# Paired causal attentions on one core: three of a group's four key blocks summed in one visit to the 32-column part of the array

## The reference

```python
x = _layernorm(x + _L0_attn_ref(x, ...))      # causal, 16 heads of 8 channels, T = 256
...
# _L2_attn_ref
scores = jnp.einsum('bthd,bshd->bhts', q, k) / jnp.sqrt(HD)
scores = scores + alibi[None]
scores = jnp.where(causal[None, None], -jnp.inf, scores)
attn = jax.nn.softmax(scores, axis=-1)
out = jnp.einsum('bhts,bshd->bthd', attn, v).reshape(Bb, Ss, Dd)
return out @ Wo + bo
```

## Time and profile before

| | |
|---|---|
| median of 3 runs | 2263.75 us (2261.84 to 2269.63) |
| profiled execution | 2265.27 us, its span 2263.3 us |
| TensorE busy | 1973.9 us, 87% |
| VectorE busy | 1460.6 us, 65% |
| ScalarE busy | 1171.9 us, 52% |
| GpSimd busy | 813.2 us, 36% |

### The profile page before, as it was taken

How to read it: one execution, slowest core, us unless ns; L and a number is a source line. 1 busy time by engine, 2 the same in 40 slices (tenths; PEclk the granted TensorE clock), 3 DMA queues, 4 the chain that set the end, 5 groups by cost and what they waited for, 6 DMA issues and landing times.

```text
span 2263.3 us, 44486 instructions
## 1 busy us (share of the span) xinstructions
PE 1973.9 (87%) x17496; PEld 1179.8 (52%) x17496; DVE 1460.6 (65%) x2920; ACT 1171.9 (52%) x1950; POOL 813.2 (36%) x1153
## 2 busy tenths in 40 slices
PE   5886689998878989998999788999899898999888
PEld 2342466666644544554665344444555665666446
DVE  5775687878768777773555776121677676767464
ACT  2575356656622444555333467322576675757432
POOL 4544343433126748343001331000545344453033
PEclk7998799999989999999999899999999999999999
DMA  4430111111234434210201220000465564655152
GB/s 130 140 103 2 25 31 28 30 33 26 63 107 127 125 98 137 59 49 1 104 1 50 88 91 20 32 0 1 154 206 175 173 208 131 207 174 168 51 114 56
DMA packets 183990, 199.10 MB, mean 88 GB/s; under 512 B 55922, under 2 KB 152486, under 8 KB 179302
## 3 DMA queue, kind: packets, MB, share of 16 engines
q1 hardware_dynamic: 183782, 196.27, 29.5%
HBM read 93.53 MB, written 92.08 MB: 82 GB/s over the span
## 4 chain that ended last, share of the span: by engine, by line
PE 34%; DVE 6%; ACT 6%; issue 3%; DMA 2%; POOL 2%; SPq 1%; DVEq 0%; ACTq 0%; POOLq 0%
PE PS L2104 5%; PE PS L357 4%; PE PS L2351 3%; PE PS L2367 3%; PE PS L1957 3%; PE PS L2339 3%; ACT AR L2509 2%; PE PS L1944 2%; PE PS L1947 2%; PE PS L2703 1%; PE PS L604 1%; PE PS L2691 1%; PE PS L2693 1%; DMA AR<-ZD 1%; PE PS L583 1%
## 5 line engine op out<-in xcount | busy, mean ns | idle before, releaser
L1282 ACT ACTIVATE AR<-PS 128x1024 f32<-128x1024 f32 x160 | 162.6, 1024 | 123.9 <-PE PS L1031 123.0
L725 ACT ACTIVATE AR<-PS 128x1024 f32<-128x1024 f32 x160 | 162.9, 1024 | 93.3 <-PE PS L583 48.0
L1135 DVE TENSOR_REDUCE AR<-PS 128x2 f32<-128x768 f32 (+1 forms) x192 | 159.9, 864 | 55.8 <-PE PS L1011 30.7
L2565 POOL TENSOR_TENSOR RA<-AR,RA 128x288 f32<-128x288 f32 x128 | 88.2, 698 | 275.4 <-DVE RA L2441 142.2
L2509 ACT ACTIVATE AR<-PS,AR 128x512 f32<-128x512 f32 x256 | 174.0, 687 | 24.2 <-DVE AR L2430 24.0
L2430 DVE TENSOR_REDUCE AR<-PS 128x2 f32<-128x1024 f32 x128 | 156.8, 1225 | 12.9
L2339 PE MATMUL PS<-AR 64*128 64x200 f32 (+2 forms) x1280 | 147.0, 354 | 2.9 <-ACT AR L2509 2.9
L1828 POOL TENSOR_TENSOR AR<-AR 128x1024 f32<-128x1024 f32 x32 | 75.4, 2358 | 174.4 <-DVE AR L1676 174.4
L2351 PEld LDWEIGHTS PS<-CC,AR 64*128 64x128 f32 x2048 | 77.8, 140 | 98.1 <-issue 76.7
L2351 PE MATMUL PS<-CC,AR 64*128 64x64 f32 x2048 | 92.3, 229 | 38.7 <-DVE AR L2436 11.7
L2339 PEld LDWEIGHTS PS<-AR 64*128 64x128 f32 x1280 | 111.3, 193 | 6.3 <-ACT AR L2509 3.2
(11 more groups left out here) (366 smaller groups left out, 4984.4 us busy)
## 6 DMA issues: line engine op xcount, KB each, us to landing
ZD<-RC SPq DMA_DIRECT2D x32, 1152.0 KB
AR<-ZD SPq DMA_DIRECT2D x32, 640.0 KB
ZP<-AR SPq DMA_DIRECT2D x128, 160.0 KB, 2.7
SP<-AR SPq DMA_DIRECT2D x40, 384.0 KB, 2.6
AR<-SP SPq DMA_DIRECT2D x128, 96.0 KB
RA<-SP SPq DMA_DIRECT2D x32, 384.0 KB
SP<-AR SPq DMA_DIRECT2D x40, 256.0 KB, 2.9
RC<-RC SPq DMA_DIRECT2D x64, 130.0 KB
```

The source lines that it names most:

```text
L725: e.activation(self.PT[m % 6], C.PS[:, 2 * s:2 * s + 2, :], ACT.Exp).then_inc(S["s_turned"].sem, 1)
L1135: i = e.tensor_reduce(nm[:, :, 4 * up + q:4 * up + q + 1], src[:, :, a:a + wd], AX, ALU.max, negate=True)
L1282: e.activation(self.PT[m % 6], C.PS[:, 2 * s:2 * s + 2, :], ACT.Exp).then_inc(S["s_turned"].sem, 1)
```

## The change

`order` puts the key blocks 1, 3 and 2 of the group before into the list together, in the step with m % 5 = 1, where they stood one each in the steps with m % 5 = 0, 1 and 2. `take` stays in the step with m % 5 = 2. The items of `post` (pieces, proj, fin, turnx) come in the steps with m % 5 = 1 and 4, where they came in those with 1 and 3. Key block 0 stays in the step with m % 5 = 4. No instruction is added or taken away, and the order of the sums is the same.

```diff
@@ -501,9 +501,9 @@
             k = m // 5
-            if m >= 5 and m % 5 < 3:
-                plan.append(("group", k - 1, (1, 3, 2)[m % 5]))
-                if m % 5 == 2:
+            if m >= 5 and m % 5 == 1:
+                plan.extend(("group", k - 1, kb) for kb in (1, 3, 2))
+            if m >= 5 and m % 5 == 2:
                     plan.append(("take", k - 1))
                     if k % 4 == 0:
                         post += [[("piece", k // 4 - 1, q)] for q in range(NT)] + [[(s, k // 4 - 1)] for s in ("proj", "fin", "turnx")]
@@ -515,7 +515,7 @@
-            elif post and (m % 5 in (1, 3) or m >= N):
+            elif post and (m % 5 in (1, 4) or m >= N):
                 plan += post.pop(0)
```

## The result

The changed kernel takes 2293.1 us (median of 4 runs, 2290.4 to 2297.7) against 2266.7 us; the ratio is 1.0125, 95% interval 1.0102 to 1.0147. It is slower by 26 us, the way that was forecast, but 12 us above the forecast of 2280.7 and 2 us above the top of its range. Measured once more in a later series it took 2292.0 us, ratio 1.0122 (1.0102 to 1.0142). The profiled execution took 2290.4 us, its span 2287.4, 24.1 more than before.

A forecast was written before the change was run, and what follows sets the result against it. TensorE was taken to bound the kernel only while each step carries filling work. Uncovered waits less saved shape changes gave +9.9 us (second stage) and +7 (first), +16.9 on 2263.75: 2280.7 us, range 2264 to 2291 for 8 in 10.

The forecast's parts named there:

- Rival 1: Whole kernel: TensorE bounds and array-shape changes count; uncovered waits stay small, 8 us gained, 2256 us; chance 0.12.
- Rival 2: Both stages: new waits only replace existing waits for maxima and normalisation stalls; about 2268 us; chance 0.14.
- Rival 3: Merged visit itself waits for exp or select, 1 us in each first-stage group; 2296 us; chance 0.08.
- The price of a group: Second-stage group: 1.4 us of uncovered waits less 0.26 saved; +1.1 us where no wait was before.
- S3: Start of the `scores` matmuls in step m % 5 = 3; second stage: 0.45 us wait for the exp.
- S4: Start of the `scores` matmuls in step m % 5 = 4; second stage: 0.59 us wait, exp behind `take`.
- k 7: Second-stage group with proj in step 3: 1.1 us, plus 0.7 as `value` behind proj needs its bank cleared.
- k 1: First second-stage group counted: ends on DMAs of the start, so 0 us.
- k 2: Second-stage group where step 3 already had a 0.32 us wait: +0.8 us.
- k 12: Second-stage group where ScalarE's normalisation stall was to take in part of the new waits: +0.3 us.
- the sum: Adding group costs over both stages: +9.9 us in the second, +7 in the first, +16.9 in total.
- the terms that I took at nothing: Second stage's first group, steps without scores at its end, and turnx and proj moved in the last group: 0 us.

## Why the prediction was right in kind and short in size

**The bound and the rivals.** That TensorE is the bound only as long as each step is filled was right. Rival 1 (the shape changes decide) is refuted by the merged visit alone (1.0085); the shape change itself was sized right, at 0.14 us a visit in the kernel with two blocks joined and 0.28 us a group in the merged one, for 0.26 forecast. The Trainium skill (TensorEngine Tiling, Key Properties) says that a change of the tiling mode drains TensorE. The rows agree in that each change taken out saves 0.14 us; that it is a drain, they do not show. What it is worth depends on who is waiting. Rival 2 (absorbed) did not come: the maxima's waits fell from 9.7 to 4.8 us in the first stage, as foretold in kind, but they were not enough, and in the second stage they rose from 3.8 to 4.4. Rival 3 did not come: no row of the merged visit waits for the select.

**The price of a group.** Forecast 1.4 us of waits (0.35, 0.45, 0.59) less 0.26, measured 1.45 (0.33, 0.65, 0.47) less 0.28: +1.17 for +1.1. S3 was dearer than said, because step 2 takes 0.73 us when bare, not 0.83, and `scores` came 0.15 us behind the exp, not 0.06; S4 was cheaper by 0.12 us. Group by group in the second stage, from the `turned` of step 0, with the forecast in brackets: k 5 and 6 +1.17 each (1.1), k 7 +1.86 (1.8), k 8 +0.22 (0.3), k 9 +1.44 (1.1), k 10 +1.17 (1.1), k 11 +0.62 (0.8), k 13 +0.42 (0.8), k 3 and 4 together +0.59 (0.7). Far off are k 1, +1.36 (0), k 2, +1.80 (0.8), and k 12, +1.37 (0.3). In the first stage the four groups with a piece grew by 4.6 us (4.8).

**Where it failed.** The step that failed is the sum: the terms that I took at nothing or at 0.3 for the places where the norm, the transfers and the stage's end set the pace, and a term that it does not have at all, stretches at a low granted clock. By part, the second stage is +4.1, +8.1 and +1.9 us for 1.5, 7.6 and 0.8, and the first stage +9.6 for 7; in the second profile +4.7, +8.9, +2.2 and +8.3.
- k 12, second stage: +1.37 us for 0.3, at a granted clock of 1.00. I took ScalarE's stall for the norm to swallow part of the new waits. It is the other way round: the length of step 0 is set by the stall, and the 384 visit that stood in it had been free. It saves 0.15 us where it left and is paid in full in step 1. The move of `fin` by one step changes what `rows` waits for (`value`'s addition is queued behind the norm on VectorE, and `rows` behind the bank), but costs little: the moved pieces alone make +0.31 us in this group, the merged visit alone +0.80.
- k 12, first stage: +3.11 us. Step 0 is again 0.15 us shorter, but behind its wait of 2.37 us the merged visit runs at the lower of the clock's two levels. Timeline of TensorE and busy time by stretch (the clock is the third number from the end):

```profile
173.62 2.79 PE L604 MATMUL PS<-AR 128*32 128x384 f32 x24
173.62:176.33 2.71, 2.71 (x26) 0.98 (x24) 1.29 (x2) 0.55 (x1) 1.36 (x4) 0.50 0.05 11
```

It takes 2.71 us to the next instruction, for 1.43 at full clock. In the second profile the same came in k 12 of the second stage, 12.74 us for 11.11, with the visit at 2.69. In the first stage the group's mean granted clock is 0.73 to 0.88 in all six profiles of the kernels with the merged visit and the work in full, and 1.00 in all five of those without it.
- The first stage: its middle part grew by 10.9 us in one profile and 6.4 in the other. Besides k 12, the group k 4 grew by 2.09 us, with the 512 visit at a granted clock of 0.51 (1.86 us to the next instruction, for 1.00).
- The start of the second stage: +4.1 us, for 1.5 forecast. k 2 took 10.16 us at a granted clock of 0.83; the kernel with the norm put back, whose order is the same up to there, has 8.99 at 1.00. So 1.2 us of it go with the clock. The rest is k 1, which waits for the transfers, and part of both may be chance, as the moved pieces' kernel shows.
- The end of the second stage: +1.9 us for 0.8 (that of k 13). The 512 visit of the last group waits 3.37 us for `take`, which ScalarE does only after the square root of the third block's norm; that norm comes one step later, behind a proj that is one step later. The moved pieces alone show the same wait, 3.23 us. I had set this against the cover that the visit gives turnx. The last merged visit behind it runs at a granted clock of 0.50 too (2.79 us for 1.50).

In sum 9.6 + 14.2 for 7 + 9.9, and some 2 us more by the medians (26.4) than by the traces (24.1), which their interval (23 to 33) takes in. The range was too narrow by 2 us; it was made from the price of a group, not from the terms taken at nothing.

That the price of an ordinary group came out so near owes something to luck, since the errors at S3 (+0.20 us) and S4 (-0.12) are of opposite sign.

The mean granted clock of the stages fell (0.92 to 0.89, and 0.98 to 0.95). Not all of this is the change's own: the kernel with two blocks joined shows 0.90 and 0.95 in one profile and 0.92 and 0.98 in the other, which has stages 1.5 and 3.2 us shorter. Its k 2 of the second stage takes 9.75 us at 0.82 and 8.22 at 1.00. What the low stretches cost the changed kernel in all, over those that the kernel before has too, stays open.

## What to carry to other kernels

When work is moved between steps of a pipeline to save a fixed cost, ask first what latency it covers where it stands: here 0.28 us a group was saved and 1.45 us of exp and maxima uncovered, and merging only as far as each step keeps some filling gave 0.14 us for nothing. Read the cost of the emptied step from a step that is already bare, one with a late engine beside it. And give a place where another engine stalls for microseconds (here a norm, with two table loads around its square root) a term of its own: work that stands in such a stall is free there and is paid in full where it is moved to, and putting the norm back does not bring that cover back.

## What the runs showed of the hardware

A bracket in TensorE's timeline understates a wait behind a matmul: at S3 the bracket says 0.49 us, the distance from start to start grew by 0.65; over a group the brackets make 0.97 us and the delays 1.45. So the busy time of the group k = 10 rose from 7.94 to 8.15 us, at a granted clock of 1.00 in both, though no matmul was added and the merged visit is shorter. This and the low clock raise TensorE's busy time by 3 us in each stage; how much each has of it is not told apart.

The same 24 matmuls of the merged visit take 1.50 us at a granted clock of 1.00 and 2.79 at 0.50. A change between the exp and the square root costs ScalarE a table load of 1.28 us each way.
